# Attention scores: the low-k term on 64 rows, two q tiles at a time in the two halves of TensorE

## The chip, the cores and the metric

One kernel on one core of a Trainium2 chip. The metric is the device time of one execution in microseconds (us). The engines named below are TensorE (PE in the rows, and PEld for its weight loads), VectorE (DVE), ScalarE (ACT), GpSimd (POOL) and the SyncE queue (SP), which issues the DMAs.

## The reference, cut to what matters

Input x is 4 x 512 x 1024. After a layer norm an attention with 16 heads of 64 columns runs on it, and its output is multiplied by a gated feed-forward branch. What concerns this change is how q, k and the scores come about:

```python
q = (hidden_states @ Wq).reshape(b, s, HEADS, HEAD_DIM)
k = (hidden_states @ Wk).reshape(b, s, HEADS, HEAD_DIM)
v = (hidden_states @ Wv).reshape(b, s, HEADS, HEAD_DIM)
...
logits = jnp.einsum('bhqd,bhkd->bhqk', q, k)      # q, k after the rotary turn
logits = jnp.where(causal, logits, MASK_VAL)
logits = logits / jnp.sqrt(jnp.float32(HEAD_DIM))
attn = jax.nn.softmax(logits, axis=-1)
out = jnp.einsum('bhqk,bhkd->bhqd', attn, v)
...
return x + attention_output * silu(ffn_output)
```

## The kernel before

The program has three stages: the feed-forward branch (to about 200 us), a loop over 32 attention steps (to about 975 us), and the output product with Wo. A step is one batch element and one pair of heads (128 columns of q, k and v). The two heads of a pair sit on partitions 0 to 63 and 64 to 127 (`pair_rows`).

TensorE multiplies in a reduced format (fp32r), so every product is made of a high and a low part of each operand: high x high, high x low and low x high. The high part is a copy with rounding (ScalarE), the low part is the float32 value minus the high part (VectorE or GpSimd).

Step s is software pipelined. TensorE runs the projections q, k, v of step s (`project`, 24 matmuls each, helper `split_matmuls`, lines 44 to 46), and between their pieces the work of steps s-1 and s-2: `v_transposes` (L1077), `scores` (L1092, L1093), `prob_transposes` (L1110) and `values` (L1123). The order is written out by hand in `step` of each engine's block, and semaphores tie the engines together. Each engine works through its own list strictly in order.

The score tile of one head is 512 queries by 512 keys, causal, so query tile t (128 queries) needs (t+1) x 128 keys: widths 128, 256, 384 and 512 for t = 0 to 3. They lie in three PSUM banks: bank 0 holds t=3, bank 1 holds t=2 at column 0 and t=0 at column 384, bank 2 holds t=1 (`SCORE_BANKS`). Before the change a stationary operand of 128 rows (`q_st`) holds high q of head h on its own 64 rows and low q on the other 64. The moving operand `k_hh` holds high k on both halves, so one matmul (L1092) gives high q x high k plus low q x high k. A second matmul (L1093) with the same stationary operand and `k_l0` (low k on the own 64 rows, zeros on the other 64) adds high q x low k. There are thus 8 matmuls a head, on all 128 rows, and `scored` counts up after each bank.

Who feeds whom, as far as the prediction needs it: GpSimd `rotate` writes the turned q and k (`rotated[0]`, `rotated[1]`); ScalarE `q_high` and `k_high` (L1266, L1272) write the high parts; VectorE `q_low` and `k_low` (L1504, L1511) the low parts and count up `qk_ready`. On VectorE, `k_low(s)` stands ahead of `pt_low_parts(2s-1, 1, (0, 1))` (L1544), and TensorE's `prob_transposes(2s-1, 1, (2,))` of the next step may start only when the first of these two has read its PSUM bank (`pt_ready`). VectorE's `maxima` (L1527) waits for `scored`; ScalarE's `exps` (L1297) follows it, then VectorE's `normalise` (L1533, L1537), then `prob_transposes`.

The feed-forward stage has one function that uses TensorE in parts: `gate` (L231) runs four matmuls with a stationary operand of 32 columns each, which write to partitions 0, 32, 64 and 96 of `ff_small`, in four rounds per call.

## Time and profile before

| | |
|---|---|
| median of 3 runs | 1139.34 us (1139.3 to 1139.48) |
| profiled execution, its own time | 1140.27 us |
| its span, first to last instruction | 1138.5 us |
| mean granted TensorE clock | 0.997 |
| TensorE busy / weight loads busy | 1107.5 us (97%) / 925.2 us (81%) |
| VectorE busy | 798.3 us (70%) |
| ScalarE busy | 639.6 us (56%) |
| GpSimd busy | 385.2 us (34%) |

The profiled execution took 0.93 us more than the median of the runs. Busy shares are averages over the stages. Ends of matmuls in the trace are modelled, and successive matmuls overlap in it, so the distance from one start to the next says what a matmul costs in a stream, not its duration.

### The profile page before, as it was taken

How to read it: one execution, taken by the hardware profiler on the slowest of the kernel's cores; microseconds unless marked ns; L12 is line 12 of the kernel's file. 1: busy time of each engine (PE TensorE's matmuls, PEld its weight loads, DVE VectorE, ACT ScalarE, POOL GpSimd, SP SyncE). 2: the span in 40 equal slices, each digit the busy share in tenths (PEclk: the TensorE clock that was granted, in tenths of full speed). 3: DMA queues.
4: the chain of work that ended last, by engine and by line, in shares of the span. 5: the costliest groups of instructions: out<-in, count | busy, mean ns of one | idle time of the engine just before them, and what ended most of it. 6: DMA issues, size and time to landing. Idle time of an engine off the chain costs nothing.

```text
span 1138.5 us, 17762 instructions
## 1 busy us (share of the span) xinstructions
PE 1107.5 (97%) x5620; PEld 925.2 (81%) x5620; DVE 798.3 (70%) x1860; ACT 639.6 (56%) x1344; POOL 385.2 (34%) x240
## 2 busy tenths in 40 slices
PE   4899999999999999999999999999999999999998
PEld 3667777888888888888888888888888887788887
DVE  6768641476767776767776677767677768899865
ACT  6545542366665666646566565666656667645341
POOL 0443646352342433334342352523424335200000
PEclk9899999999999999999999999999999999999999
DMA  9526133220202202021460202202022014586764
GB/s 368 209 93 241 55 94 111 75 65 11 64 9 74 64 10 64 9 64 49 172 221 9 64 18 64 64 9 64 9 74 64 10 64 168 188 282 219 235 212 148
DMA packets 88719, 116.40 MB, mean 102 GB/s; under 512 B 3440, under 2 KB 69104, under 8 KB 87664
## 3 DMA queue, kind: packets, MB, share of 16 engines
q1 hardware_dynamic: 88688, 116.01, 30.4%
q8 instruction: 16, 0.26, 0.1%
q14 instruction: 15, 0.12, 0.0%
HBM read 82.44 MB, written 33.55 MB: 102 GB/s over the span
## 4 chain that ended last, share of the span: by engine, by line
PE 87%; DVE 6%; ACT 3%; issue 1%; POOL 1%; DMA 1%; SPq 0%; DVEq 0%; POOLq 0%; ACTq 0%
PE at_proj L44 17%; PE at_proj L46 17%; PE at_proj L45 17%; PE at_out L1123 7%; PE at_pt L1110 6%; PE ff_z_ps L286 5%; PE at_score L1092 4%; PE at_score L1093 3%; POOL ff_xs_lo L669 1%; PE at_pt L44 1%; PE at_pt L46 1%; PE at_pt L45 1%; PE at_proj L1077 1%; PE at_score L44 1%; PE at_score L45 1%
## 5 line engine op out<-in xcount | busy, mean ns | idle before, releaser
L44 PE MATMUL at_proj<-xn_hi,w_hi 128*128 128x512 f32 x824 | 333.6, 405 | 1.6 <-POOL w_lo L1813 0.8
L46 PE MATMUL at_proj<-xn_hi,w_lo 128*128 128x512 f32 x824 | 322.8, 392 | 0.0
L45 PE MATMUL at_proj<-xn_lo,w_hi 128*128 128x512 f32 x824 | 321.3, 390 | 0.0
L46 PEld LDWEIGHTS at_proj<-xn_hi,w_lo 128*128 128x128 f32 x824 | 154.6, 188 | 34.5
L1797 POOL TENSOR_TENSOR at_turning<-at_turning,rope_table 128x512 f32<-128x512 f32 x64 | 82.8, 1294 | 289.4 <-DVE at_turning L1499 289.4
L44 PEld LDWEIGHTS at_proj<-xn_hi,w_hi 128*128 128x128 f32 x824 | 154.9, 188 | 29.1 <-issue 1.2
L45 PEld LDWEIGHTS at_proj<-xn_lo,w_hi 128*128 128x128 f32 x824 | 155.3, 188 | 27.5
L1297 ACT ACTIVATE at_prob<-at_score,at_neg_max 128x512 f32<-128x512 f32 (+3 forms) x256 | 133.5, 526 | 71.2 <-DVE at_neg_max L1527 70.8
L1805 POOL TENSOR_TENSOR w_lo<-w_stage,w_hi 128x1024 fp32r<-128x1024 f32 x45 | 114.4, 2558 | 162.9 <-ACT w_hi L1259 162.9
L1306 ACT ACTIVATE at_pt_hi<-at_pt 128x512 fp32r<-128x512 f32 (+1 forms) x192 | 94.0, 524 | 99.7 <-PE at_pt L1110 98.9
L1544 DVE TENSOR_TENSOR at_pt_lo<-at_pt,at_pt_hi 128x512 fp32r<-128x512 f32 (+1 forms) x192 | 112.1, 598 | 42.1 <-ACT at_pt_hi L1306 41.1
L1527 DVE CUSTOM_DVE_ANT_0 at_score<-at_score,at_causal 128x512 f32<-128x512 f32 (+3 forms) x256 | 120.8, 514 | 1.0
L1110 PE MATMUL at_pt<-ident,at_prob 128*128 128x128 f32 x640 | 91.7, 274 | 0.8 <-DVE at_pt_lo L1544 0.6
L1313 ACT ACTIVATE at_low_half<-at_out 64x512 f32<-64x512 f32 x64 | 37.9, 592 | 96.8 <-PE at_out L1123 96.0
L1801 POOL TENSOR_TENSOR at_rotated<-at_turning 128x512 f32<-128x512 f32 x64 | 82.8, 1293 | 7.3 <-POOL at_turning L1797 4.4
L1511 DVE TENSOR_TENSOR at_qk<-at_rotated,at_qk 64x512 fp32r<-64x512 f32 x64 | 45.1, 705 | 56.4 <-ACT at_qk L1272 56.0
L286 PE MATMUL ff_z_ps<-sign_t,ff_xs_hi 128*128 128x512 f32 x256 | 83.4, 407 | 0.8 <-POOL ff_xs_lo L669 0.8
L1537 DVE TENSOR_SCALAR at_prob<-at_prob,at_inv_sum 128x256 f32<-128x256 f32 (+3 forms) x256 | 82.0, 384 | 2.3
L1272 ACT ACTIVATE at_qk<-at_rotated 64x512 fp32r<-64x512 f32 x128 | 80.5, 629 | 1.8 <-POOL at_rotated L1801 0.2
L286 PE MATMUL ff_z_ps<-sign_t,ff_xs_lo 128*128 128x512 f32 x256 | 81.4, 399 | 0.0
L1092 PE MATMUL at_score<-at_qk 128*128 128x512 f32 (+3 forms) x256 | 80.5, 328 | 0.0
L1110 PEld LDWEIGHTS at_pt<-ident,at_prob 128*128 128x128 f32 x640 | 73.0, 141 | 6.6 <-DVE at_pt_lo L1544 1.6
(214 smaller groups left out, 1924.9 us busy)
## 6 DMA issues: line engine op xcount, KB each, us to landing
w_stage<-_attn_hidden_states_dram SPq DMA_DIRECT2D x17, 512.0 KB, 6.4
z_store<-z SPq DMA_DIRECT2D x16, 512.0 KB, 2.8
w_stage<-in_L_attn_Wq_dram SPq DMA_DIRECT2D x16, 512.0 KB, 3.8
w_stage<-in_L_attn_Wk_dram SPq DMA_DIRECT2D x16, 512.0 KB, 5.1
w_stage<-in_L_attn_Wv_dram SPq DMA_DIRECT2D x16, 512.0 KB, 6.2
att_store<-at_att_t SPq DMA_DIRECT2D x32, 256.0 KB, 2.0
at_turning<-z_store SPq DMA_DIRECT2D x16, 512.0 KB, 5.4
w_stage<-in_L_attn_Wo_dram SPq DMA_DIRECT2D x12, 512.0 KB, 4.3
```

The lines of the kernel that those rows point to most:

```text
L44: pe.matmul(out, sh, mh, start=first, stop=False, skip_group_check=reopened)
L45: pe.matmul(out, sh, ml, start=False, stop=False, skip_group_check=reopened)
L46: return pe.matmul(out, sl, mh, start=False, stop=final, skip_group_check=reopened)
L286: last = pe.matmul(z_ps[n % 2][:, o, :], part[:, k, tok], keep["sign_t"][:, k, o * HALF:(o + 1) * HALF], start=(k == 0 and part is xs_hi), ...
L1092: pe.matmul(out, q, k_hh[parity][h][:, 0:width], start=True, stop=False)
L1110: last = pe.transpose(pt_ps[u % 2][:, dst:dst + P], prob[h][:, src:src + P], keep["ident"][:])
L1297: last = act.activation(prob[h][:, P_COL[t]:P_COL[t] + width], score_ps[bank][:, col:col + width], ACT.Exp, scale=-1.0, bias=neg_max[h][:, ...
L1306: act.activation(pt_hi[h][:, 512 * u:512 * u + PT_WIDTH[u]], pt_ps[u % 2][:, 0:PT_WIDTH[u]], ACT.Copy).then_inc(pt_high, 1)
L1527: last = dve.tensor_tensor_reduce(out=row, in0=row, in1=causal[:, (QT - 1 - t) * P:SEQ], scale=-1.0, scalar=FAR, op0=ALU.add, op1=ALU.min, ...
L1544: dve.tensor_tensor(pt_lo[h][:, cols], pt_ps[u % 2][:, 0:PT_WIDTH[u]], raw(pt_hi[h][:, cols]), ALU.subtract).then_inc(pt_ready, 1)
L1797: pool.tensor_tensor(swapped[c][:], swapped[c][:], rope[:, 2 * c + 1, :], ALU.mult).then_inc(rot_a, 1)
L1805: pool.tensor_tensor(w_lo[m][:], w_raw[m], raw(w_hi[m][:]), ALU.subtract).then_inc(w_ready[m], 1)
```

## The change

- `scores` issues the four matmuls with `k_hh` first (widths 512, 384, 128, 256), all on 128 rows, and then four matmuls for high q x low k on 64 rows only. Query tiles 3 and 1 take them on the head's own 64 rows (`q_st` own rows with `k_own`), tiles 2 and 0 on the other 64 rows (`q_other` with `k_other`). `scored` counts up only in this second half. In bank 1 only the tile at column 0 starts a group.
- `q_other` is new: ScalarE copies the query tiles 0 and 2 of high q of each head onto the other 64 rows, two instructions of 64 x 256 per step, behind `q_high`.
- `k_low` writes low k to the head's own rows (`k_own`, 64 x 512, as before) and then, in two more instructions of 64 x 384, to the other rows (`k_other`).
- The zeros in `k_l0`, four memsets before the loop, and the semaphore `zeroed` are gone.
- GpSimd's `rotate` waits for `qk_ready` at 2s for both q and k, where it waited for 2s-1 for q.

```diff
--- before.py
+++ after.py
@@ -735,7 +735,12 @@
             v_t = lsb("at_v_t", [P, SEQ], F32)
 
             qk = lsb("at_qk", [P, 2, 6, SEQ], F32R)
-            q_st, k_hh, k_l0 = ([[qk[:, p, c + h, :] for h in range(2)] for p in range(2)] for c in (0, 2, 4))
+            q_st, k_hh = ([[qk[:, p, c + h, :] for h in range(2)] for p in range(2)] for c in (0, 2))
+
+            k_own, k_other = ([qk[:, p, c, :] for p in range(2)] for c in (4, 5))
+            q_other = lsb("at_q_other", [P, 2, 2 * P], F32R)
+            OTHER_COL = {0: 0, 2: P}
+            OTHER_KEYS = 3 * P
 
             v_hl = [lsb(f"at_v_hl{p}", [P, QT, 4, HEAD_DIM], F32R) for p in range(2)]
             neg_max = [lsb(f"at_neg_max{h}", [P, QT], F32) for h in range(2)]
@@ -775,7 +780,6 @@
         w_high, w_ready, rope_in = keep["w_high"], keep["w_ready"], keep["rope_in"]
 
         xn_in, xn_ok = sem("at_xn_in"), keep["xn_ok"]
-        zeroed = sem("at_zeroed")
         projected = sem("at_projected")
         rot_read, rot_a, rot_done = sem("at_rot_read"), sem("at_rot_a"), sem("at_rot_done")
         high_done, qk_ready = sem("at_high_done"), sem("at_qk_ready")
@@ -1080,17 +1084,25 @@
             def scores(a, h, parity):
                 n = 2 * a + h
                 pe.wait_ge(qk_ready, 2 * a + 2)
-                if not later(a, 2):
-                    pe.wait_ge(zeroed, 4)
+                own, other = pair_rows[h], pair_rows[1 - h]
                 for bank, tiles in enumerate(SCORE_BANKS):
                     if later(n, 1):
                         pe.wait_ge(expd, 3 * (n - 1) + bank + 1)
                     for t, col in tiles:
                         width = (t + 1) * P
-                        out = score_ps[bank][:, col:col + width]
-                        q = q_st[parity][h][:, t * P:(t + 1) * P]
-                        pe.matmul(out, q, k_hh[parity][h][:, 0:width], start=True, stop=False)
-                        last = pe.matmul(out, q, k_l0[parity][h][:, 0:width], start=False, stop=True)
+                        pe.matmul(score_ps[bank][:, col:col + width], q_st[parity][h][:, t * P:(t + 1) * P],
+                                  k_hh[parity][h][:, 0:width], start=(col == 0), stop=False, skip_group_check=True)
+                for bank, tiles in enumerate(SCORE_BANKS):
+                    for t, col in tiles:
+                        width = (t + 1) * P
+                        if t in OTHER_COL:
+                            q = q_other[other, parity, OTHER_COL[t]:OTHER_COL[t] + P]
+                            k = k_other[parity][other, 0:width]
+                        else:
+                            q = q_st[parity][h][own, t * P:(t + 1) * P]
+                            k = k_own[parity][own, 0:width]
+                        last = pe.matmul(score_ps[bank][:, col:col + width], q, k, start=False, stop=True,
+                                         skip_group_check=True)
                     last.then_inc(scored, 1)
 
             def prob_transposes(n, h, uses):
@@ -1265,6 +1277,9 @@
                 for h, rows in enumerate(pair_rows):
                     last = act.activation(q_st[b][h][rows, :], rotated[0][rows, :], ACT.Copy)
                 last.then_inc(high_done, 1)
+                for h, rows in enumerate(pair_rows):
+                    act.activation(q_other[pair_rows[1 - h], b, :].rearrange("p (t n) -> p t n", t=2),
+                                   rotated[0][rows, :].rearrange("p (t a n) -> p t a n", t=2, a=2)[:, :, 0, :], ACT.Copy)
 
             def k_high(s, b, h):
                 act.wait_ge(rot_done, 2 * s + 2)
@@ -1508,7 +1523,10 @@
             def k_low(s, b):
                 dve.wait_ge(high_done, 2 * s + 2)
                 for h, rows in enumerate(pair_rows):
-                    last = dve.tensor_tensor(k_l0[b][h][rows, :], rotated[1][rows, :], raw(k_hh[b][h][rows, :]), ALU.subtract)
+                    dve.tensor_tensor(k_own[b][rows, :], rotated[1][rows, :], raw(k_hh[b][h][rows, :]), ALU.subtract)
+                for h, rows in enumerate(pair_rows):
+                    last = dve.tensor_tensor(k_other[b][pair_rows[1 - h], 0:OTHER_KEYS], rotated[1][rows, 0:OTHER_KEYS],
+                                             raw(k_hh[b][h][rows, 0:OTHER_KEYS]), ALU.subtract)
                 last.then_inc(qk_ready, 1)
 
             def v_low(a, parity):
@@ -1576,9 +1594,6 @@
                     merge(s - 1, 2 * s - 2, 0, 1 - b)
 
             dve.wait_ge(keep["z_add"], BATCH * QT)
-            for p in range(2):
-                dve.memset(raw(k_l0[p][0][HEAD_DIM:P, :]), 0.0).then_inc(zeroed, 1)
-                dve.memset(raw(k_l0[p][1][0:HEAD_DIM, :]), 0.0).then_inc(zeroed, 1)
             def wo_lo(k):
                 dve.wait_ge(wo_high, k + 1)
                 dve.tensor_tensor(wo_part[k][PLO], wo_raw[:, k % 3, :], raw(wo_part[k][PHI]), ALU.subtract).then_inc(wo_low_dve, 1)
@@ -1797,7 +1812,7 @@
                 pool.tensor_tensor(swapped[c][:], swapped[c][:], rope[:, 2 * c + 1, :], ALU.mult).then_inc(rot_a, 1)
                 pool.wait_ge(rot_a, 2 * s + c + 1)
                 if later(s, 1):
-                    pool.wait_ge(qk_ready, 2 * s + c - 1)
+                    pool.wait_ge(qk_ready, 2 * s)
                 pool.tensor_tensor(rotated[c][:], swapped[c][:], turned[c][:], ALU.add).then_inc(rot_done, 1)
 
             def weights_low(idx, m):
```

TensorE's list, at the first call of `scores` inside the loop. The rows with `at_out` are the end of `values` and the last row is the first matmul of the k projection. Before:

```order
L1123 MATMUL at_out<-at_pt_lo,at_v_hl 128x128
L1087 ISA [waits at_qk_ready]
L1092 MATMUL at_score<-at_qk 128x512 [waits at_expd]
L1093 MATMUL at_score<-at_qk 128x512
L1087 REGISTER_ALU
L1092 MATMUL at_score<-at_qk 128x384 [waits at_expd]
L1093 MATMUL at_score<-at_qk 128x384
L1092 MATMUL at_score<-at_qk 128x128
L1093 MATMUL at_score<-at_qk 128x128
L1087 REGISTER_ALU
L1092 MATMUL at_score<-at_qk 128x256 [waits at_expd]
L1093 MATMUL at_score<-at_qk 128x256
```

The same place of the changed kernel, whose line numbers differ (L1093 is now the product with high k, L1104 the one with low k):

```order
L1135 MATMUL at_out<-at_pt_lo,at_v_hl 128x128
L1090 ISA [waits at_qk_ready]
L1093 MATMUL at_score<-at_qk 128x512 [waits at_expd]
L1090 REGISTER_ALU
L1093 MATMUL at_score<-at_qk 128x384 [waits at_expd]
L1093 MATMUL at_score<-at_qk 128x128
L1090 REGISTER_ALU
L1093 MATMUL at_score<-at_qk 128x256 [waits at_expd]
L1104 MATMUL at_score<-at_qk 128x512
L1104 MATMUL at_score<-at_qk,at_q_other 128x384
L1104 MATMUL at_score<-at_qk,at_q_other 128x128
L1104 MATMUL at_score<-at_qk 128x256
```

The number of matmuls and their widths are the same; the four low-k products have moved behind all four high-k products.

VectorE's list around `k_low` (the rows with `at_prob` are the end of `normalise`, those with `at_pt_lo` are `pt_low_parts`, the last is `merge`). Before:

```order
L1537 TENSOR_SCALAR at_prob<-at_prob,at_inv_sum 128x512
L1511 TENSOR_TENSOR at_qk<-at_rotated,at_qk 64x512 [waits at_high_done]
L1511 TENSOR_TENSOR at_qk<-at_rotated,at_qk 64x512
L1544 TENSOR_TENSOR at_pt_lo<-at_pt,at_pt_hi 128x512 [waits at_pt_high] x2
L1552 TENSOR_TENSOR at_att_t<-at_out,at_low_half 64x512 [waits at_half_copied]
```

The same place of the changed kernel:

```order
L1555 TENSOR_SCALAR at_prob<-at_prob,at_inv_sum 128x512
L1526 TENSOR_TENSOR at_qk<-at_rotated,at_qk 64x512 [waits at_high_done]
L1526 TENSOR_TENSOR at_qk<-at_rotated,at_qk 64x512
L1528 TENSOR_TENSOR at_qk<-at_rotated,at_qk 64x384 x2
L1562 TENSOR_TENSOR at_pt_lo<-at_pt,at_pt_hi 128x512 [waits at_pt_high] x2
L1570 TENSOR_TENSOR at_att_t<-at_out,at_low_half 64x512 [waits at_half_copied]
```

Two instructions of 64 x 384 now stand between `k_low` and `pt_low_parts`.

## Rows read from the trace of the kernel before

**Rows 1.** Page, part 1: busy time, share of the span, instructions.

```profile
PE 1107.5 (97%) x5620; PEld 925.2 (81%) x5620; DVE 798.3 (70%) x1860; ACT 639.6 (56%) x1344; POOL 385.2 (34%) x240
```

**Rows 2.** Page, part 4: the chain that ended last, share of the span by engine.

```profile
PE 87%; DVE 6%; ACT 3%; issue 1%; POOL 1%; DMA 1%; SPq 0%; DVEq 0%; POOLq 0%; ACTq 0%
```

**Rows 3.** Windows: the loop without its ends; busy us and count per engine, clock.

```profile
230.00:950.00 720.00, 720.00 (x3810) 617.97 (x3809) 511.59 (x1337) 439.06 (x1002) 269.48 (x166) 1.00 0.18 56
```

**Rows 4.** Timeline of TensorE: scores of both heads begin, the second whole; start, duration, what.

```profile
510.21 0.45 PE L1092 MATMUL at_score<-at_qk 128*128 128x512 f32 x1
...
517.01 0.39 PE L1092 MATMUL at_score<-at_qk 128*128 128x512 f32 x1
...
517.46 0.33 PE L1092 MATMUL at_score<-at_qk 128*128 128x384 f32 x1
...
517.81 0.22 PE L1092 MATMUL at_score<-at_qk 128*128 128x128 f32 x1
517.87 0.27 PE L1093 MATMUL at_score<-at_qk 128*128 128x128 f32 x1
517.98 0.33 PE L1092 MATMUL at_score<-at_qk 128*128 128x256 f32 x1
518.15 0.28 PE L1093 MATMUL at_score<-at_qk 128*128 128x256 f32 x1
518.27 1.03 PE L1110 MATMUL at_pt<-ident,at_prob 128*128 128x128 f32 x8
```

**Rows 5.** Timeline of the weight loads, end of the same call.

```profile
517.92 0.19 PEld L1092 LDWEIGHTS at_score<-at_qk 128*128 128x128 f32 x1
518.03 0.19 PEld L1093 LDWEIGHTS at_score<-at_qk 128*128 128x128 f32 x1
```

**Rows 6.** Timeline of TensorE around the third call of gate.

```profile
147.35 0.63 PE L286 MATMUL ff_z_ps<-sign_t,ff_xs_lo 128*128 128x512 f32 x2
147.91 1.92 PE L231 MATMUL ff_small<-xn_full,ff_gate_raw 128*32 128x512 f32 x16
149.77 0.73 PE L286 MATMUL ff_z_ps<-sign_t,ff_xs_hi 128*128 128x512 f32 x2
150.34 0.63 PE L286 MATMUL ff_z_ps<-sign_t,ff_xs_lo 128*128 128x512 f32 x2
```

**Rows 7.** Timeline of the weight loads around the same call.

```profile
147.91 0.16 PEld L231 LDWEIGHTS ff_small<-xn_full,ff_gate_raw 128*32 128x32 f32 x8 [0.37 <-issue]
148.37 0.13 PEld L231 LDWEIGHTS ff_small<-xn_full,ff_gate_raw 128*32 128x32 f32 x4 [0.30 <-issue]
148.80 0.13 PEld L231 LDWEIGHTS ff_small<-xn_full,ff_gate_raw 128*32 128x32 f32 x4 [0.30 <-issue]
149.76 0.30 PEld L286 LDWEIGHTS ff_z_ps<-sign_t,ff_xs_hi 128*128 128x128 f32 x2 [0.84 <-issue]
```

**Rows 8.** Timeline of VectorE: k_low, pt_low_parts, v_low, maxima of head 0.

```profile
502.83 1.39 DVE L1511 TENSOR_TENSOR at_qk<-at_rotated,at_qk 64x512 fp32r<-64x512 f32 x2 [1.65 <-ACT at_qk L1272]
504.25 1.29 DVE L1544 TENSOR_TENSOR at_pt_lo<-at_pt,at_pt_hi 128x512 fp32r<-128x512 f32 x2
...
506.85 0.69 DVE L1516 TENSOR_TENSOR at_v_hl<-at_proj,at_v_hl 128x512 fp32r<-128x512 f32 x1 [0.72 <-ACT at_v_hl L1286]
...
511.76 0.70 DVE L1527 CUSTOM_DVE_ANT_0 at_score<-at_score,at_causal 128x512 f32<-128x512 f32 x1
```

**Rows 9.** Timeline of the weight loads: prob_transposes behind v_transposes.

```profile
505.91 0.25 PEld L1110 LDWEIGHTS at_pt<-ident,at_prob 128*128 128x128 f32 x2
```

**Rows 10.** Groups by form, 300 to 900 us, VectorE: busy, mean ns.

```profile
L1511 DVE TENSOR_TENSOR at_qk<-at_rotated,at_qk 64x512 fp32r<-64x512 f32 x50 | 34.3, 686 | 41.6 <-ACT at_qk L1272 41.3
...
L1544 DVE TENSOR_TENSOR at_pt_lo<-at_pt,at_pt_hi 128x256 fp32r<-128x256 f32 x50 | 21.0, 420 | 33.5 <-ACT at_pt_hi L1306 33.5
```

**Rows 11.** Timeline of ScalarE behind q_high.

```profile
518.90 1.09 ACT L1306 ACTIVATE at_pt_hi<-at_pt 128x512 fp32r<-128x512 f32 x2 [1.80 <-PE at_pt L1110]
```

**Rows 12.** Groups by form, 300 to 900 us, ScalarE: a copy of 256 columns.

```profile
L1306 ACT ACTIVATE at_pt_hi<-at_pt 128x256 fp32r<-128x256 f32 x50 | 19.0, 380 | 19.8 <-PE at_pt L1110 19.8
```

## Prediction

> **What bounds the kernel now.** I read part 1 of the page first: TensorE is busy 97% of the span, VectorE 70%, ScalarE 56% [rows 1]. The chain that ended last is 87% TensorE [rows 2], so this is the engine whose list sets the end. Then the windows: from 230 to 950 us, 720 us of loop, TensorE is busy for all 720.00 us, with the clock at 1.00 of 2.4 GHz, while VectorE is busy 511.59 us and ScalarE 439.06 us [rows 3]. In the loop nothing but the length of TensorE's own list counts, and the other two engines matter only where they would make it wait. There are 32 steps and two calls of `scores` a step, 64 calls. So 0.1 us on a call is 6.4 us on the kernel.
>
> **One call of scores now.** In a stream the cost of a matmul is the distance to the next start. The call starts at 517.01 and what follows starts at 518.27, so it costs 1.26 us [rows 4]. The two 512-wide ones take 0.45 us together, the 384-wide ones 0.35 us. The last four, 128, 128, 256 and 256 wide, take 518.27 - 517.81 = 0.46 us. Weight loads behind each other start 0.11 us apart (517.92, 518.03) [rows 5], so four loads are 0.44 us, and these four matmuls go at the pace of their loads, not of their columns. A narrow matmul therefore costs about 0.11 us here.
>
> **The high half of the new call.** 512 wide 0.225, 384 wide 0.175, then 128 and 256 wide at 0.11 each: 0.62 us. The whole old call less this, 0.64 us, is what the low-k matmuls cost today.
>
> **The low half of the new call** has no row before: no matmul in this trace runs on 64 rows. The nearest rows are those of `gate`, which runs four stationary operands of 32 columns side by side. Four things are read there. First, the parts do run together: 16 matmuls of 512 columns start at 147.91 and the next work starts at 149.77 [rows 6], and a new round of loads comes each 0.43 to 0.46 us (147.91, 148.37, 148.80 [rows 7]), not after four matmuls' time. Second, loads for different parts are issued almost together, 8 loads in 0.16 us. Third, the way in: the last full matmul begins at 147.35 + 0.23 = 147.58, would hand over at 147.81, and the first part load starts only at 147.91. In a stream of full matmuls the load is started while the matmul before it still streams (the load of 518.03 [rows 5] serves the matmul of 518.15 [rows 4]); here TensorE's load side stood idle 0.37 us "issue", that is without a semaphore to wait for, and the array ran 0.10 us dry. Fourth, the way out: rounds of 0.43 us put the end of the last one at 147.91 + 4 x 0.435 = 149.65, and the full-width load comes at 149.76, again after 0.84 us of "issue" idle time, so 0.11 us dry; then the load itself, 0.11 us, is exposed (150.34 - 149.77 = 0.57 us for two matmuls instead of 0.46). I count a switch from full array to part as 0.10 us dry plus 0.11 us for an exposed 128-column load, and back as 0.11 + 0.11 us. Both together are 0.43 us, paid once in each call.
>
> Between the switches the own half streams 512 and 256 columns (0.225 + 0.11 = 0.34 us), the other half 384 and 128 columns beside it (0.29 us), which is hidden. The low half costs 0.34 + 0.43 = 0.77 us, the call 0.62 + 0.77 = 1.39 us. Against 1.26 us that is +0.13 us, and 64 x 0.13 = +8 us.
>
> The bounds of this term: without any switching cost the call is 0.62 + 0.34 = 0.96 us, 64 x -0.30 = -19 us. With the switching cost and no overlap of the halves it is 0.62 + 0.64 + 0.43 = 1.69 us, 64 x 0.43 = +28 us. I take the switches at the price of rows 6 and 7 because the load side stood idle with no semaphore to wait for, on both sides of `gate`, and the width of the part in use is what differs there. That the row concerns parts of columns, and the change makes parts of rows, is the weak point.
>
> The Trainium skill, TensorEngine Tiling (Array Packing), Key Properties, says that changing the tiling mode, as against the tile, drains TensorE. By that rule the trace agrees with the 0.10 and 0.11 us dry [rows 6, 7], and the sum keeps both; without it the sum would lose 27 us. The Trainium skill, TensorE: Matmul & The Clock Gate, Part 3 (Packing small matmuls), gives 3.07 times for four row parts and a few ns between parts, and prices no switch. By that page alone the call would be the 0.96 us of the lower bound; no run here shows it for rows yet.
>
> **What VectorE gets.** Two instructions of 64 x 384 a step. A subtraction of 256 columns takes 420 ns, one of 512 columns 686 ns [rows 10], which is 1.04 ns a column, so 384 columns are 553 ns, with 10 ns between them 1.13 us a step. Behind them waits `pt_low_parts`. It starts now at 504.25 and its first of two is done 0.69 us later, at 504.94 [rows 8]. It would be done at 506.07, and with about 0.05 us for the semaphore TensorE can start the load of the transposes at 506.12. Today that load starts at 505.91 [rows 9]. `k_low` itself is released by ScalarE, which is released by TensorE's v projection, and no call of scores lies between that projection and these transposes, so the distance does not change with the first term. TensorE waits 0.21 us in each of 31 steps: +6.5 us. Bounds: 0 if the new pieces take 0.42 us each, +15 us at 0.69 us each (0.21 + 2 x 0.135 = 0.48 us a step). Next in VectorE's list is `v_low`, with 0.72 us idle ahead of it [rows 8], so it starts 0.4 us late, at 507.3, and the third `pt_lo` behind it is done by 507.3 + 0.69 + 0.42 = 508.4. `values`, of the same eight widths as a call of scores and so 1.26 us long, needs that at 510.21 - 1.26 = 508.95 [rows 4]: covered.
>
> **What ScalarE gets.** Two copies of 64 x 256, about 0.38 us each by the nearest form [rows 12], so 0.8 us behind `q_high`, in front of `pt_hi` at 518.90, ahead of which ScalarE is idle 1.80 us [rows 11]. That idle time hides it; 0 us. Without it the copies would cost up to 0.8 us a step, 25 us. GpSimd's low weights start 0.8 us later and are waited for half a step later at the earliest. `rotate` for q waits for `k_low` of the step before; VectorE runs that ahead of the `rotate_read` for which GpSimd waits anyway, so 0.
>
> **Scored comes later** for bank 0: 0.62 + 0.21 + 0.23 us into the call and the array's latency of about 0.17 us (0.39 less 0.225 [rows 4]), 1.2 us in place of 0.6 us. The call for head 0 starts at 510.21 [rows 4] and its first maximum at 511.76 [rows 8], because `merge` stands before it on VectorE. 510.2 + 1.2 = 511.4 is still early: 0 us. The four memsets before the loop lie beside TensorE's first projections: 0 us.
>
> **Sum.** +8 + 6.5 = +14.5 us on a span of 1138.5 and on the profiled execution's 1140.27, which gives 1154.8; that execution was 0.93 us over the median of the runs, so 1153.8. I say 1153.
>
> **Rivals.**
> - The switch is free or nearly so for row parts (the loads go ahead as in a full stream). The call is 0.96 us, -19 us, the wait on VectorE stays: -19 + 6.5 = -12.5 us, 1127. It speaks for it that loads inside a round of `gate` are prefetched (8 at once). Against it, the two idle stretches of the load side in rows 7. It decides from a switch in and out below 0.30 - 0.10 = 0.20 us (the 0.10 being the wait, 6.5/64). This is the rival on the other side. Chance 0.26.
> - Half the switch (one way hidden, 0.2 us): call 1.17 us, -6 + 6.5 = 0, 1139. Chance 0.12, split over all three signs.
> - The halves do not overlap, since both write to the same partitions of PSUM, though in different banks, where the parts of `gate` write to different partitions. +28 + 6.5 = +34 us, 1174; with cheap switches 1146. This is also the rival in which the change does not do what it says. Chance 0.14.
> - My forecast, both switches paid: 0.48.
>
> **Chances and range.** Faster by over 0.2% takes the first rival and a third of the second, 0.30; within 0.2% (2.3 us, about what a measurement tells apart) 0.05; slower 0.65. The likeliest case's own range is 1146 to 1162: 1153.8 less 6.5 or plus 8.5 us, the bounds of the VectorE term. Cases of both signs hold much of the chance, so the range goes down to 1122, the first rival with the wait at a few us less, and up to 1160.
>
> **What would show it.** In the changed kernel's timeline of TensorE a call should take about 1.39 us; the load side should show an "issue" gap ahead of the first 64-row load and ahead of the first full load behind the call; the starts of the 512-wide and 384-wide low matmuls should lie within 0.05 us. TensorE should be idle some 0.2 us ahead of `prob_transposes` (2,) in each step, released by VectorE's `at_pt_lo`. It is wrong if the loads of the 64-row matmuls start one matmul ahead (then 1127), or if the low starts are 0.17 us or more apart (then 1174).

## Result and the profile after

The changed kernel takes 1151.37 us (median of 4 runs, 1150.88 to 1152.08) against 1139.32 us before on the same chip: ratio 1.0107, 95% interval 1.009 to 1.0125, 12.05 us slower. The forecast was 1153 us, slower. A second measurement of the same kernel, on another occasion (below), gave 1150.97 us, ratio 1.0098, interval 1.0082 to 1.0113.

The profiled execution took 1150.88 us, its span 1149.1 us, 10.6 us more than before. Part 1 of the page of the changed kernel, as in [rows 1]:

```profile
PE 1118.2 (97%) x5620; PEld 908.4 (79%) x5620; DVE 829.4 (72%) x1920; ACT 664.9 (58%) x1408; POOL 377.7 (33%) x240
```

The number of matmuls is the same; VectorE has 60 instructions more and ScalarE 64. The windows show that the loop is bound as before, as in [rows 3]:

```profile
230.00:950.00 720.00, 720.00 (x3759) 594.65 (x3758) 534.85 (x1377) 454.96 (x1045) 255.49 (x162) 1.00 0.18 55
```

In the same 720 us TensorE gets through 3759 matmuls, where it got through 3810, at the same clock. Its list takes longer, though TensorE is counted busy throughout; the busy time does not say why.

**The two calls of scores** in the timeline of TensorE, as in [rows 4]: head 0 with the projection behind it, then head 1 with the transposes behind it. Columns: start us, duration us, engine, line, what; "x4" merges the four matmuls with high k, "x2" the two on the other half:

```profile
513.32 0.85 PE L1093 MATMUL at_score<-at_qk 128*128 128x512 f32 x4
514.11 0.50 PE L1104 MATMUL at_score<-at_qk 64*128 64x512 f32 x1
...
514.44 0.28 PE L1104 MATMUL at_score<-at_qk 64*128 64x256 f32 x1
514.65 0.50 PE L44 MATMUL at_proj<-xn_hi,w_hi 128*128 128x512 f32 x1
514.99 0.40 PE L45 MATMUL at_proj<-xn_lo,w_hi 128*128 128x512 f32 x1
...
520.25 0.79 PE L1093 MATMUL at_score<-at_qk 128*128 128x512 f32 x4
520.96 0.49 PE L1104 MATMUL at_score<-at_qk 64*128 64x512 f32 x1
520.97 0.50 PE L1104 MATMUL at_score<-at_qk,at_q_other 64*128 64x384 f32 x2
521.29 0.27 PE L1104 MATMUL at_score<-at_qk 64*128 64x256 f32 x1
521.50 1.09 PE L1122 MATMUL at_pt<-ident,at_prob 128*128 128x128 f32 x8
522.35 0.48 PE L44 MATMUL at_proj<-xn_hi,w_hi 128*128 128x512 f32 x1
```

The 512-wide matmul on one half and the 384-wide one on the other start 0.01 us apart, so the halves do run together. The low half takes 521.50 - 520.96 = 0.54 us, where the prediction has 0.34 us without switches. The timeline of the weight loads for the same call:

```profile
520.02 0.81 PEld L1093 LDWEIGHTS at_score<-at_qk 128*128 128x128 f32 x4
520.96 0.18 PEld L1104 LDWEIGHTS at_score<-at_qk 64*128 64x128 f32 x1
520.96 0.18 PEld L1104 LDWEIGHTS at_score<-at_qk,at_q_other 64*128 64x128 f32 x1
521.07 0.19 PEld L1104 LDWEIGHTS at_score<-at_qk 64*128 64x128 f32 x1
521.07 0.19 PEld L1104 LDWEIGHTS at_score<-at_qk,at_q_other 64*128 64x128 f32 x1
521.50 0.86 PEld L1122 LDWEIGHTS at_pt<-ident,at_prob 128*128 128x128 f32 x8 [0.24 <-issue]
```

Inside the low half the loads go well: two start at the same moment, and the next two 0.11 us later, while the first matmuls stream. At the edges they do not. The first 64-row load starts 0.13 us after the loads of 520.02 to 520.83 have ended and with the matmul that it serves, not one matmul ahead, and the load for the transposes comes only at 521.50, after 0.24 us in which the load side waited for nothing that the profile shows ("issue"). That is the signature of [rows 7].

The starts show where the time goes. In the call for head 1:

- The high half takes 520.96 - 520.25 = 0.71 us, where 0.62 us was worked out: 0.09 us dry on the way in.
- From the 512-wide to the 256-wide matmul of the same half it is 521.29 - 520.96 = 0.33 us in place of 0.225: 0.11 us, the first load exposed.
- From there to the transposes it is 521.50 - 521.29 = 0.21 us in place of 0.11: 0.10 us dry on the way back.
- The transposes then take 522.35 - 521.50 = 0.85 us, before 519.06 - 518.27 = 0.79: 0.06 us, what is exposed of their load.

In the call for head 0 the first three are the same within 0.01 us (its high half is 0.79 us long, but this call was 0.07 us longer than the other before the change too). The projection behind it takes 514.99 - 514.65 = 0.34 us to the next start where it has 0.23 us in a stream: 0.11 us. So a pair of switches costs some 0.42 us with a projection behind it and some 0.36 us with transposes behind it. The call itself is not longer than before (1.25 us for head 1, before 1.26): what it saves by the overlap pays for the first three parts, and the fourth falls on what follows. (The lists of TensorE's order ahead of the prediction end with the call itself; the projection's matmul that they announce as their last row is the one of 514.65.)

What the change costs for each call in the end is read from start to start over calls and what follows. From the call for head 0 to the call for head 1 it is 520.25 - 513.32 = 6.93 us, before 517.01 - 510.21 = 6.80 [rows 4]: +0.13 us. From the call for head 1 to the first projection behind the eight transposes it is 522.35 - 520.25 = 2.10 us, before 519.06 - 517.01 = 2.05: +0.05 us. The row of before that [rows 4] does not have:

```profile
519.06 0.47 PE L44 MATMUL at_proj<-xn_hi,w_hi 128*128 128x512 f32 x1
```

**The wait behind k_low.** The timeline of VectorE, as in [rows 8]:

```profile
505.75 1.39 DVE L1526 TENSOR_TENSOR at_qk<-at_rotated,at_qk 64x512 fp32r<-64x512 f32 x2 [1.64 <-ACT at_qk L1287]
507.15 1.12 DVE L1528 TENSOR_TENSOR at_qk<-at_rotated,at_qk 64x384 fp32r<-64x384 f32 x2
508.31 1.29 DVE L1562 TENSOR_TENSOR at_pt_lo<-at_pt,at_pt_hi 128x512 fp32r<-128x512 f32 x2
```

and the weight load of the transposes that need the first `at_pt_lo`, as in [rows 9]:

```profile
509.05 0.20 PEld L1122 LDWEIGHTS at_pt<-ident,at_prob 128*128 128x128 f32 x2 [0.18 <-DVE at_pt_lo L1562]
```

Before, that load had no wait in brackets. It now starts 509.05 - 508.52 = 0.53 us behind the first v transpose, before 505.91 - 505.59 = 0.32 us:

```profile
505.59 0.60 PE L1077 MATMUL at_proj<-ident,at_v_t 128*128 128x128 f32 x4
506.02 0.38 PE L1110 MATMUL at_pt<-ident,at_prob 128*128 128x128 f32 x2
506.16 0.47 PE L44 MATMUL at_proj<-xn_hi,w_hi 128*128 128x512 f32 x1
```

and in the changed kernel:

```profile
508.52 0.60 PE L1081 MATMUL at_proj<-ident,at_v_t 128*128 128x128 f32 x4
509.05 0.44 PE L1122 MATMUL at_pt<-ident,at_prob 128*128 128x128 f32 x2
509.25 0.47 PE L44 MATMUL at_proj<-xn_hi,w_hi 128*128 128x512 f32 x1
```

The group of waits from 300 to 900 us counts them (waited for: us in total, times, longest):

```profile
PEld at_pt L1122 <- issue: 6.0, 25, 0.2
PEld at_proj L44 <- issue: 5.9, 24, 0.2
PEld at_pt L1122 <- DVE at_pt_lo L1562: 4.3, 24, 0.2
```

The first two lines are the way back from 64 rows, once for each head, and the third is VectorE, 0.18 us a step on the load side. From the v transposes to the matmul behind the third-bank transposes the step grew by 0.16 us (509.25 - 508.52 = 0.73, before 506.16 - 505.59 = 0.57). A whole step went from 24.19 us (starts of the v transposes at 505.59 and 529.78) to 24.53 us (508.52 and 533.05). The 0.34 us are 0.13 + 0.05 for the two calls and 0.16 for the wait.

From the first v transposes to those of the last step the trace grew by 10.15 us: 29 steps of 0.34 us, and 0.16 and 0.15 us for the first and the last distance. The part ahead of the loop is 0.96 us shorter (first v transposes at 215.81 us, before 216.77), and the part behind them 1.40 us longer (175.98 us, before 174.58), which makes the 10.6 us of the span. That start lies anywhere from 215.46 (`e2_k_copies`) to 217.55 us (`e1_order`) in traces of kernels that change nothing ahead of the loop, so the 0.96 us need not come from the change. The 1.40 us were not traced to their parts.

### The profile page after: what moved, and what is told of

The parts are those of the page before. It is cut to its first block, busy times and chain, and to the rows that moved or that the text cites. A ratio compares the mean times of both kernels' runs of the same rounds, so it can differ in the third digit from the quotient of the medians.

```text
span 1149.1 us, 17885 instructions
## 1 busy us (share of the span) xinstructions
PE 1118.2 (97%) x5620; PEld 908.4 (79%) x5620; DVE 829.4 (72%) x1920; ACT 664.9 (58%) x1408; POOL 377.7 (33%) x240
## 4 chain that ended last, share of the span: by engine, by line
PE 87%; DVE 6%; ACT 3%; issue 1%; POOL 1%; DMA 1%; SPq 0%; DVEq 0%; POOLq 0%; ACTq 0%
PE at_proj L44 17%; PE at_proj L46 17%; PE at_proj L45 17%; PE at_pt L1122 7%; PE at_out L1135 7%; PE ff_z_ps L286 5%; PE at_score L1093 4%; PE at_score L1104 3%; POOL ff_xs_lo L669 1%; PE at_pt L46 1%; PE at_pt L45 1%; PE at_pt L44 1%; PE at_proj L1081 1%; PE at_score L44 1%; PE at_score L46 1%
## 5 line engine op out<-in xcount | busy, mean ns | idle before, releaser
L1820 POOL TENSOR_TENSOR w_lo<-w_stage,w_hi 128x1024 fp32r<-128x1024 f32 x45 | 107.3, 2397 | 173.7 <-ACT w_hi L1271 173.7
L1122 PE MATMUL at_pt<-ident,at_prob 128*128 128x128 f32 x640 | 95.4, 280 | 0.9 <-DVE at_pt_lo L1562 0.6
L1122 PEld LDWEIGHTS at_pt<-ident,at_prob 128*128 128x128 f32 x640 | 70.2, 141 | 19.8 <-DVE at_pt_lo L1562 7.5
L1135 PE MATMUL at_out<-at_pt_hi,at_v_hl 128*128 128x512 f32 (+3 forms) x256 | 76.5, 310 | 1.9 <-DVE at_pt_lo L1562 1.2
```

The source lines that it names most:

```text
L1122: last = pe.transpose(pt_ps[u % 2][:, dst:dst + P], prob[h][:, src:src + P], keep["ident"][:])
L1135: last = pe.matmul(out_ps[:, kt * P:SEQ], v, part[h][:, cols], start=(kt == 0 and part is pt_hi), stop=(kt == QT - 1 and part is pt_lo))
L1820: pool.tensor_tensor(w_lo[m][:], w_raw[m], raw(w_hi[m][:]), ALU.subtract).then_inc(w_ready[m], 1)
```

## The experiments

The kernels `e1_order`, `e2_k_copies`, `e3_q_copies`, `e6_alternate` and `e8_one_switch` start from the kernel before, the others from the changed one. Ratios are to the kernel before on the same chip, with their 95% interval. Before was 1139.54 us beside e1, e2, e3 and e8, 1139.44 us beside e4 to e7, 1139.46 us beside e9 to e11.

The total holds the two ends of the program as well. What one step costs is read from the starts of the v transposes in each trace, as the mean of 28 steps from the third on:

| kernel | one step, us | over before |
|---|---|---|
| before, `e3_q_copies` | 24.19 | |
| `e1_order` | 24.17 | -0.03 |
| `e2_k_copies` | 24.37 | +0.17 |
| `e4_no_k_copies`, `e9_scalar_copies`, `e10_late_apart` | 24.35 | +0.16 |
| changed, `e11_changed_again` | 24.53 | +0.34 |
| `e8_one_switch` | 24.91 | +0.72 |
| `e5_own_half` | 24.95 | +0.76 |
| `e6_alternate` | 27.10 | +2.91 |
| `e7_late_copies` | 24.35 and 25.93 by turns | |

The wait alone (+0.17) and the 64-row matmuls alone (+0.16) add up to the changed kernel (+0.34) within 0.01 us.

**The order alone** (`e1_order`): four high, then four low matmuls, all on 128 rows.

```diff
-                        pe.matmul(out, q, k_hh[parity][h][:, 0:width], start=True, stop=False)
-                        last = pe.matmul(out, q, k_l0[parity][h][:, 0:width], start=False, stop=True)
-                    last.then_inc(scored, 1)
+                        pe.matmul(out, q, k_hh[parity][h][:, 0:width], start=(col == 0), stop=False, ...)
+                for bank, tiles in enumerate(SCORE_BANKS):
+                    for t, col in tiles:
+                        last = pe.matmul(out, q, k_l0[parity][h][:, 0:width], start=False, stop=True, ...)
+                    last.then_inc(scored, 1)
```

> The kernel before with only the order of a call of scores changed: four high-k matmuls, then four low-k matmuls, all on 128 rows with the zero-padded low k, and scored counted in the second half. My theory: the order costs nothing; the widths are the same, each narrow matmul still costs about 0.11 us, bank 0 is still ready ahead of the first maximum: 1139 us, within 1.5. Rival: part of the 12 us comes from the order itself (scored later, VectorE and ScalarE late): 1142 to 1150.

Measured: 1139.22 us, ratio 0.9999 (0.999 to 1.0008). The order, and the later `scored` with it, costs nothing.

**VectorE's copies alone** (`e2_k_copies`): into a spare tile behind `k_low`.

```diff
+                for h, rows in enumerate(pair_rows):
+                    last = dve.tensor_tensor(k_spare[pair_rows[1 - h], :], rotated[1][rows, 0:3 * P],
+                                             raw(k_hh[b][h][rows, 0:3 * P]), ALU.subtract)
                 last.then_inc(qk_ready, 1)
```

> The kernel before plus the two VectorE instructions of 64 x 384 behind low k, written to a spare tile that nobody reads. My theory: the transposes of the third bank wait about 0.16 us in each of 31 steps, as in the changed kernel's trace: +5 us, 1144.5. Rival: the wait of the changed kernel comes from elsewhere (ScalarE copies, later scores), the pieces alone are hidden: 1139 to 1140.

Measured: 1145.38 us, ratio 1.0057 (1.0044 to 1.007), +5.8 us. The wait shows in the trace as in the changed kernel (300 to 900 us):

```profile
PEld at_pt L1112 <- DVE at_pt_lo L1549: 4.7, 25, 0.2
```

**ScalarE's copies alone** (`e3_q_copies`): the two copies of 64 x 256 into a spare tile, and `rotate`'s wait at 2s.

> The kernel before plus the two ScalarE copies of 64 x 256 behind high q, written to a spare tile that nobody reads, and GpSimd's later wait. My theory: hidden in ScalarE's idle time: 1139 us, within 1. Rival: they push the weights' low parts and the high k later and TensorE waits: 1142 or more.

Measured: 1139.61 us, ratio 1.0001 (0.9993 to 1.001). Hidden.

**One switch a call** (`e8_one_switch`):

```diff
+                        rows = own if t == 1 else slice(0, P)
-                        last = pe.matmul(out, q, k_l0[parity][h][:, 0:width], start=False, stop=True)
+                        last = pe.matmul(out, q[rows, :], k_l0[parity][h][rows, 0:width], start=False, stop=True)
```

> The kernel before with one of its eight matmuls a call, low k of query tile 1 (256 wide), on the head's own 64 rows instead of 128 rows with zeros: one way into the 64-row shape and one way back per call, no copies, no overlap, nothing else. My theory: the pair of switches costs 0.3 to 0.43 us, 64 times: +19 to +28 us, 1163 us, and the load side shows an idle gap called issue on both sides of that matmul. Rival: a 64-row matmul among full ones costs nothing extra, the changed kernel loses elsewhere: 1139 us.

Measured: 1160.81 us, ratio 1.0191 (1.0178 to 1.0204), +21.3 us: 21.3 / 64 = 0.33 us for one way in and back. The step says 0.72 / 2 = 0.36 us; the total holds the ends too, where a call costs less: the last distance between v transposes did not grow (22.86 us, before 22.85). One call of its TensorE timeline (L1095 is the low product):

```profile
518.62 0.33 PE L1094 MATMUL at_score<-at_qk 128*128 128x256 f32 x1
518.88 0.38 PE L1095 MATMUL at_score<-at_qk 64*128 64x256 f32 x1
519.20 0.50 PE L44 MATMUL at_proj<-xn_hi,w_hi 128*128 128x512 f32 x1
```

The same two 256-wide matmuls took 518.27 - 517.98 = 0.29 us before [rows 4] and take 0.58 us here, though the second now uses half the rows. The rest lies in the first projection behind it, which takes 0.33 us to the next start in place of 0.23. From the call for head 0 to that for head 1 the kernel needs 7.18 us (before 6.80), from there to the projection behind the transposes 2.39 us (before 2.05): the way back into transposes is cheaper by 0.04 us here as well. The loads on both sides start late, each some 0.13 us behind the end of the load before it, but with so short a gap the view names no "issue" wait, which the expectation had asked for:

```profile
518.56 0.19 PEld L1094 LDWEIGHTS at_score<-at_qk 128*128 128x128 f32 x1
518.88 0.18 PEld L1095 LDWEIGHTS at_score<-at_qk 64*128 64x128 f32 x1
519.19 0.19 PEld L44 LDWEIGHTS at_proj<-xn_hi,w_hi 128*128 128x128 f32 x1
```

**Without VectorE's copies** (`e4_no_k_copies`): `k_other` is zeroed once before the loop.

> The changed kernel without the low k copies in the loop; the tile that they fill is set to zero once before the loop, so high q x low k is left out for query tiles 0 and 2. My theory: the wait of 0.16 us a step goes: 1151.4 less 5, 1146 us. Rival: that wait is of no consequence, since TensorE would wait or slow down elsewhere: 1151.

Measured: 1145.02 us, ratio 1.005 (1.0037 to 1.0064). The wait is worth 6.4 us of the changed kernel's 1151.37, and what is left, 5.6 us or 0.087 us a call, is the 64-row matmuls alone. That the copied half is zero here does not matter to the time: `e9_scalar_copies` and `e10_late_apart`, which compute the whole result, have the same step of 24.35 us.

**One half only** (`e5_own_half`): all four low matmuls on the own 64 rows, no copies.

```diff
-                        if t in OTHER_COL:
-                            q = q_other[other, parity, OTHER_COL[t]:OTHER_COL[t] + P]
-                            k = k_other[parity][other, 0:width]
-                        else:
-                            q = q_st[parity][h][own, t * P:(t + 1) * P]
-                            k = k_own[parity][own, 0:width]
+                        q = q_st[parity][h][own, t * P:(t + 1) * P]
+                        k = k_own[parity][own, 0:width]
```

> The changed kernel with all four low-k matmuls on the head's own 64 rows, so no second half is used, and without both kinds of copies. My theory: the halves do overlap in the changed kernel and save 0.28 us a call, so without overlap the low half takes 0.63 us and both switches: 1151.4 less 5 plus 18, 1164 us. Rival: the halves do not overlap, the loss of the changed kernel is that: 1146 us.

Measured: 1162.86 us, ratio 1.0207 (1.0191 to 1.0222). Against `e4_no_k_copies` the missing overlap costs 17.8 us, 0.28 us a call. So the overlap of the halves is real and worth 0.28 us (0.30 us by the steps, 24.95 less 24.35 for two calls), and it does not pay for the switches.

**Four switches a call** (`e6_alternate`): each low matmul on the own 64 rows, in the old order.

> The kernel before with each of the four low-k matmuls of a call on the own 64 rows, in the old order (high, low, high, low), so four ways in and four back a call; no copies. My theory: three more pairs of switches than a call with the low half in one piece, at 0.3 to 0.43 us each: 1164 plus 58 to 83 us, about 1235 us. Rival: the drain is paid once per call or by the width, or hidden under wide matmuls: below 1190 us.

Measured: 1229.64 us, ratio 1.0796 (1.0779 to 1.0812), +90.2 us, 0.352 us for each of the 256 pairs of switches (0.36 us by the steps). The price of a pair hardly depends on how many there are. Beside what a matmul costs at full rows it does depend on the width:

```profile
525.65 0.50 PE L1094 MATMUL at_score<-at_qk 64*128 64x512 f32 x1
526.08 0.45 PE L1093 MATMUL at_score<-at_qk 128*128 128x384 f32 x1
526.46 0.44 PE L1094 MATMUL at_score<-at_qk 64*128 64x384 f32 x1
526.83 0.33 PE L1093 MATMUL at_score<-at_qk 128*128 128x128 f32 x1
527.09 0.32 PE L1094 MATMUL at_score<-at_qk 64*128 64x128 f32 x1
527.34 0.38 PE L1093 MATMUL at_score<-at_qk 128*128 128x256 f32 x1
```

A 512-wide matmul now takes 0.43 us to the next start, the 384-wide ones 0.38 and 0.37 us, where a stream of full ones has 0.225 and 0.175 us: some 0.2 us at each change, in either direction. The 128-wide ones take 0.26 and 0.25 us, where a narrow one costs 0.11 us in the old call, so there a change adds only 0.15 us.

**Copies later on VectorE** (`e7_late_copies`): meant to be the mended version.

```diff
                 if later(s, 1):
                     pt_low_parts(2 * s - 1, 1, (0, 1))
+                k_copies(b)
+                if later(s, 1):
                     merge(s - 1, 2 * s - 2, 0, 1 - b)
```

> The changed kernel with the low k copies moved behind the two pt_low parts on VectorE, with a semaphore of their own for scores and GpSimd; the result is the same. My theory: the transposes wait no longer, the switch price stays: 1146 us, still slower than before by 6 to 7. Rival: the copies push v_low and the third pt_low too far and cost the same there: 1150 to 1152.

Measured: 1172.11 us, ratio 1.0285 (1.0271 to 1.0299), 21 us worse than the kernel that it should mend. It is neither the 1146 us of the theory nor the 1150 to 1152 us of the rival. The timeline of VectorE has the two copies at 3.23 us in every second step, against 1.12 us in the others:

```profile
488.58 1.29 DVE L1567 TENSOR_TENSOR at_pt_lo<-at_pt,at_pt_hi 128x512 fp32r<-128x512 f32 x2
489.90 3.23 DVE L1533 TENSOR_TENSOR at_qk<-at_rotated,at_qk 64x384 fp32r<-64x384 f32 x2
493.16 0.68 DVE L1575 TENSOR_TENSOR at_att_t<-at_out,at_low_half 64x512 f32<-64x512 f32 x1
```

In those steps GpSimd starts the low parts of the next weights at that moment:

```profile
490.02 5.33 POOL L1828 TENSOR_TENSOR w_lo<-w_stage,w_hi 128x1024 fp32r<-128x1024 f32 x2 [6.98 <-ACT w_hi L1273]
```

and TensorE's `values` then waits for the third `at_pt_lo` (300 to 900 us, 12 of 24 steps):

```profile
PE at_out L1137 <- DVE at_pt_lo L1567: 16.0, 12, 1.3
```

From this came a theory of its own, that the two engines stop each other, and two kernels to test it.

**Late copies kept apart from GpSimd** (`e10_late_apart`):

```diff
                 rotate(s, 1)
                 if b == 1:
+                    pool.wait_ge(copied, s + 1)
                     weights_low(i + 1, 1)
```

> The kernel with the late copies (1172 us), and GpSimd's low parts of the k and v weights held back until the copies are done, so that the two engines do not run together there. Theory formed on the trace of the late copies: in every second step one 64 x 384 subtraction took 2.67 us in place of 0.55 because it ran beside a GpSimd instruction with two inputs in SBUF; kept apart it takes 0.55 us and the time is about 1146 us. Rival: the place of the copies in VectorE's list is what costs, whatever GpSimd does: 1165 or more.

Measured: 1148.6 us, ratio 1.0079 (1.0066 to 1.0093). Of the 26.6 us between `e7_late_copies` and the expected 1145 to 1146, 23.5 are gone by holding another engine back for a microsecond, so the place of the copies was not at fault. The loop's step is 24.35 us, as in `e4_no_k_copies`. Against that kernel 3.6 us are left, and they stand behind the last v transposes (178.8 us to the end, 175.4 in `e4_no_k_copies`), which the edit does not reach: there TensorE's `scores` is held up once by copies that again run beside GpSimd.

```profile
971.97 2.87 DVE L1533 TENSOR_TENSOR at_qk<-at_rotated,at_qk 64x384 fp32r<-64x384 f32 x2
```

```profile
971.50 2.36 POOL L1832 TENSOR_TENSOR xn_lo<-w_stage,xn_hi 128x1024 fp32r<-128x1024 f32 x1 [2.13 <-ACT xn_hi L1335]
```

```profile
PE at_score L1095 <- issue: 2.3, 1, 2.3
```

**Copies on ScalarE** (`e9_scalar_copies`): `k_other` from `k_own`, in the next step.

```diff
+            def k_copies(a, parity):
+                act.wait_ge(qk_ready, 2 * a + 2)
+                for h, rows in enumerate(pair_rows):
+                    last = act.activation(k_other[parity][pair_rows[1 - h], 0:OTHER_KEYS],
+                                          raw(k_own[parity][rows, 0:OTHER_KEYS]), ACT.Copy)
+                last.then_inc(copied, 1)
```

> The changed kernel with the copies of low k made by ScalarE (two of 64 x 384 from the own half's low k, in the next step, in front of its copy of the low half, where ScalarE is idle for about 3 us), not by VectorE; the result is the same. My theory: VectorE's list is as short as before, so the wait of the transposes goes, and the switch price of the 64-row matmuls alone is left, as without the copies: 1145 us, slower than before by 0.5%. Rival: work of this size behind low k costs the same on any engine, or more, since scores waits for it: 1150 or more.

Measured: 1146.36 us, ratio 1.0059 (1.0045 to 1.0073). With the whole of the work done and nobody waiting for VectorE this form is 4.6 us faster than the changed kernel beside it, and still 6.9 us slower than before. It is 1.3 us over `e4_no_k_copies`, with the same step; the distance between the last two v transposes is 23.93 us here and 22.83 us there, and why was not looked into.

**The yardstick** (`e11_changed_again`), beside the last two:

> The changed kernel once more, on the same chip as the two above, as the yardstick: 1151.4 us, within 1.

Measured: 1150.97 us, ratio 1.0098 (1.0082 to 1.0113).

No version here beats the kernel before. By the steps one pair of switches costs 0.36 to 0.38 us (`e8_one_switch`, `e6_alternate`, `e5_own_half`), the overlap that it buys gives 0.30 us, and the 0.08 us between them are the step of `e4_no_k_copies` (+0.16 us for two calls). By the totals it is 0.33 to 0.35 us against 0.28. Either way a form with one pair of switches for one call loses.

## Why the prediction was right

- **What bounds the loop.** TensorE's list, before and after: busy 720.00 of 720 us in both.
- **The switch**, +8 us in the sum, is the step that decided the sign. The rows of `gate` gave 0.43 us for a pair; measured directly it is 0.36 us (the steps of `e8_one_switch` and `e6_alternate`). A call was forecast at +0.13 us and cost 0.13 and 0.05 us more for the two heads, so the term came to 5.6 us in place of 8 (`e4_no_k_copies`). The mechanism was right: the four parts of the pair, 0.10 dry and 0.11 for a load on the way in, 0.11 dry and 0.11 for a load on the way back, are all in the trace, at 0.10 to 0.11 us each in the call for head 0. The term was too large because it was read from a way back into 512-wide matmuls alone. The call for head 0 goes back into such and met the forecast; the call for head 1 goes back into transposes and cost 0.08 us less. Of this, 0.05 us are the load on the way back, 0.06 us in place of 0.11, and `e8_one_switch` has nearly the same difference between its two calls. That transposes lose less because they go at the pace of their loads anyway fits this and the 128-wide matmuls of `e6_alternate`; no run isolates it. The call was also expected to be 1.39 us long; it is 1.25 us for head 1 and 1.33 us for head 0, as long as before, because the last part falls on what follows.
- **The overlap of the halves** was taken at 0.30 us (1.26 less 0.96) and measured at 0.28 us by the totals and 0.30 by the steps. The rival that they do not overlap is out: starts 0.01 us apart, and `e5_own_half`.
- **The rival of the free switch** is out by the late loads and by `e8_one_switch`. (Of the two "issue" gaps that were forecast the view names the one on the way back; the one on the way in is 0.13 us.) The weak point named in the prediction, that `gate` makes parts of columns and the change parts of rows, did not matter for the sign: both have a price, of nearly the same size (0.43 and 0.36 to 0.42 us).
- **The wait on VectorE**, +6.5 us from 0.21 us a step: 0.16 us a step, 5.8 us alone (`e2_k_copies`), 6.4 us the other way round (`e4_no_k_copies`). The pieces took 554 ns where 553 were worked out, the first `at_pt_lo` was done at 508.31 + 0.69 = 509.00 and the load followed at 509.05, so the 0.05 us for the semaphore held, and the load did start 0.21 us later behind the v transposes (0.53 against 0.32 us). What failed is the step from the load to TensorE's list: before, the load of 505.91 stood 0.11 us ahead of the matmul that it serves (506.02), and this slack took up part of the delay. The list grew by 0.16 us.
- **ScalarE's copies** took 0.42 us each, not 0.38, and were hidden (`e3_q_copies`, ratio 1.0001).
- **The later scored** costs nothing (`e1_order`, 0.9999).
- The parts add up: 5.6 for the 64-row matmuls and 5.8 for the wait are 11.4 of the 12.05 us. Both terms of the forecast were too large, by 2.4 and 0.7 us, so the 1153 us came from no errors that cancel.
- **A slip in the range.** The likeliest case's own range, 1153.8 less 6.5 or plus 8.5 us, is 1147 to 1162 us, not 1146, and the stated range ends below it, at 1160. Nothing hung on it.

The Trainium skill, TensorEngine Tiling (Array Packing), Key Properties, says that a change of tiling mode drains TensorE. The trace agrees, and gives out and back a size, the exposed loads included: 0.36 to 0.38 us in a step of these kernels. The Trainium skill, TensorE: Matmul & The Clock Gate, Part 3, says that matmuls on different row groups run together, a few ns apart. Here they start 0.01 us apart; the trace agrees. The second page alone would have forecast a gain, which no run here shows.

## What to carry to other kernels

Splitting the array pays only if the work in one visit saves more than the way in and back; here a visit would have to save more than 0.36 to 0.38 us and saved 0.30. A visit that served the calls of both heads would save twice as much for one price; by these numbers that would be a gain, but no run here tried it, and what it would do to the banks and the order of the calls is open. Look for an existing place in the trace where the engine changes its shape, and read the load side there: a first load that starts with its matmul and not ahead of it, on either side, with no semaphore behind it, is the sign. The size is read from the distances of starts, through to the second matmul behind the way back, and not from the gap: in `e8_one_switch` the gaps are 0.13 us each and the pair costs 0.36 us. A piece of work put in front of a hand-over costs only what it exceeds the slack by (1.12 us of copies, 0.16 us of wait), so read the slack to the hundredth before moving it, and look at what the other engines do at the new place as well.

## What the hardware showed that I had not expected

A VectorE subtraction with both inputs in SBUF stopped in these traces while GpSimd worked on SBUF inputs. 64 x 384 took 0.55 us alone and up to 2.67 us beside GpSimd's 128 x 1024 subtraction, which itself takes some 2.4 us (the group of these subtractions in `e7_late_copies`: min, median, max in ns):

```profile
L1533 DVE TENSOR_TENSOR at_qk<-at_rotated,at_qk x64: 551/554/2674, 216.7 to 997.6; 64x384 fp32r<-64x384 f32 x64
```

It is a stop and not a slow-down: in the rows of `e10_late_apart` above, GpSimd's instruction ends at 971.50 + 2.36 = 973.86 and the two copies at 974.84, 0.98 us later, and alone the two take 1.12 us. GpSimd loses as well: its two subtractions in `e7_late_copies` took 5.33 us.

`pt_low_parts`, with one input in PSUM, ran beside the same GpSimd instruction at its usual 0.69 us in the changed kernel, and the same copies on ScalarE left the step at the 24.35 us that it has without them. The Trainium skill, SBUF — State Buffer, Who interferes with whom, says this: a VectorE instruction with two SBUF inputs contends with a GpSimd instruction that reads SBUF, one with at most one, outside the modes that use both ports, does not. The trace agrees, and `e10_late_apart` shows that it was the cause. It is also what the place of the copies in the changed kernel avoids: directly behind `k_low` they end 0.34 us ahead of GpSimd's start.
